# Graph attention, layer 1: the ELU's and the residual's sums on GpSimd, row terms by transfers, maxima over more tiles, and a mask operation over two key tiles

## The reference, cut to what matters

```python
Wh = jnp.einsum('bnf,fo->bno', h, W)
s_i = Wh @ a[:Fout, 0]
s_j = Wh @ a[Fout:, 0]
e = leaky_relu(s_i[:, :, None] + s_j[:, None, :], negative_slope=0.2)
e = jnp.where(mask, e, -jnp.inf)          # mask: adj > 0, or i == j
attention = softmax(e, axis=-1)
h_prime = jnp.einsum('bij,bjo->bio', attention, Wh)
x = _layernorm(x + elu(h_prime))
```

## Time and profile before

| | us |
|---|---|
| median of 3 runs (lowest, highest) | 3980.1 (3978.75, 3983.96) |
| the profiled execution | 3980.02 |
| its span | 3978.2 |
| VectorE busy | 3254.2 (82%) |
| TensorE busy | 3643.7 (92%) |
| ScalarE busy | 2520.5 (63%) |
| GpSimd busy | 2064.1 (52%) |

### The profile page before, as it was taken

One profiled execution on the slowest core, in us unless ns is written; L12 is line 12 of the kernel. 1 busy time (PEld: TensorE's weight loads), 2 busy tenths in 40 slices (PEclk: granted clock), 3 DMA queues, 4 the chain that ended last, 5 costly groups with the idle time before them and its releaser, 6 DMA issues. The chain is left out here.

```text
span 3978.2 us, 135900 instructions
## 1 busy us (share of the span) xinstructions
PE 3643.7 (92%) x57428; PEld 2511.2 (63%) x57428; DVE 3254.2 (82%) x3989; ACT 2520.5 (63%) x3554; POOL 2064.1 (52%) x1068
## 2 busy tenths in 40 slices
PE   6999999999999999999999999942998998999898
PEld 2656756655756655665665675522776777777777
DVE  6786887787788688688788778857989989889897
ACT  3666666666666666666666666622677676776777
POOL 1786787777678687678677768831101011011010
PEclk9999999999999999999999999976999999999999
DMA  6010010010010001001001000042111110110101
GB/s 216 3 37 16 14 40 14 19 35 19 14 40 14 14 19 40 14 14 40 18 15 35 19 14 19 19 164 78 39 43 33 44 54 24 52 54 22 33 28 37
DMA packets 106692, 145.28 MB, mean 37 GB/s; under 512 B 3792, under 2 KB 87632, under 8 KB 104016
## 3 DMA queue, kind: packets, MB, share of 16 engines
q1 hardware_dynamic: 104816, 135.80, 10.2%
q10 hardware_dynamic: 1248, 0.40, 0.1%
HBM read 102.63 MB, written 33.55 MB: 34 GB/s over the span
## 5 line engine op out<-in xcount | busy, mean ns | idle before, releaser
L277 POOL TENSOR_TENSOR psums<-probs 128x1024 f32<-128x1024 f32 x512 | 1288.8, 2517 | 626.7 <-ACT probs L381 624.4
L381 ACT ACTIVATE probs<-probs 128x1024 f32<-128x1024 f32 x1024 | 1083.5, 1058 | 812.8 <-DVE probs L857 791.2
L493 PE MATMUL ctx_ps<-probs,v_rows 64*32 64x512 f32 x16256 | 1477.1, 590 | 11.7 <-DVE seg_ctx L780 10.3
L857 DVE SCALAR_TENSOR_TENSOR probs<-sc_ps,clip_hi 128x1024 f32<-128x1024 f32 x1024 | 1225.0, 1216 | 217.6 <-PE sc_ps L480 206.6
L480 PE MATMUL sc_ps<-q_cols,k_cols 64*32 64x512 f32 x16384 | 1205.0, 592 | 43.9 <-DVE probs L857 43.3
L1324 PE MATMUL out_ps<-wh,e 128*128 128x257 f32 x4096 | 963.7, 388 | 166.0 <-DVE e L1466 157.2
L1324 PEld LDWEIGHTS out_ps<-wh,e 128*128 128x128 f32 x4096 | 777.5, 193 | 326.6 <-DVE e L1466 117.9
L493 PEld LDWEIGHTS ctx_ps<-probs,v_rows 64*32 64x32 f32 x16256 | 664.0, 106 | 289.9 <-issue 190.6
L480 PEld LDWEIGHTS sc_ps<-q_cols,k_cols 64*32 64x32 f32 x16384 | 533.8, 106 | 333.9 <-issue 212.2
L1153 POOL TENSOR_TENSOR rstd<-var_eps,minus_half 128x4 f32<-128x4 f32 x32 | 68.4, 2138 | 1069.6 <-DVE var_eps L1426 1069.6
L487 PE MATMUL den_ps<-psums,ones 64*32 64x512 f32 x4064 | 598.3, 594 | 17.9 <-DVE seg_ctx L780 11.2
(11 more groups left out here) (97 smaller groups left out, 3356.1 us busy)
## 6 DMA issues: line engine op xcount, KB each, us to landing
x_cols<-in_xT SPq DMA_DIRECT2D x8, 2048.0 KB, 7.9
probs<-in_adjT SPq DMA_DIRECT2D x16, 1024.0 KB, 8.4
x_rows<-in_x SPq DMA_DIRECT2D x32, 512.0 KB, 4.1
x<-res SPq DMA_DIRECT2D x32, 512.0 KB, 2.9
x_in<-x SPq DMA_DIRECT2D x8, 2048.0 KB, 10.3
x_res<-x SPq DMA_DIRECT2D x32, 512.0 KB, 4.7
out<-h SPq DMA_DIRECT2D x32, 512.0 KB, 3.2
e<-in_adjT SPq DMA_DIRECT2D x8, 1024.0 KB, 7.8
```

The source lines that it names most:

```text
L277: pool.tensor_tensor(psums[:, q % 2, pair, :], probs[:, (SJ * q) % RING, pair, :], probs[:, (SJ * q + 1) % RING, pair, :], ALU.add).then_i ...
L381: act.activation(probs[:, n % RING, pair, :], probs[:, n % RING, pair, :], ACT.Exp, scale=DH ** -0.5).then_inc(s_exp, 1)
L493: return pe.matmul(ctx_ps[quad(h), z, :], v_rows[head_rows(r), n % JB, at:at + QUAD], probs[head_rows(r), n % RING, h, :], start=start, st ...
L857: dve.scalar_tensor_tensor(out=probs[:, n % RING, pair, :], in0=sc_ps[:, p, :, :], scalar=-LIM, in1=clip_hi[:, j, c * CW:(c + 1) * CW][:, ...
```

## The change

```diff
-    AHEAD = 3
+    AHEAD = 4
+    LARGER_AHEAD = 2
-    TU, WU, SU = KB * NC, JB, NC
-    uses_at = [1 + u for u in range(TU)] + [10 + 27 * j // JB for j in range(JB)] \
-        + [37 + 2 * c for c in range(NC)]
-    TAKEN = 4
+    TU, WU = KB * NC, JB
+    uses_at = [1 + u for u in range(TU)] + [9 + 27 * j // JB for j in range(JB)]
+    TAKEN = 3
-    LATE = 3
+    LATE = 2
+    EARLY = 2
     def max_at(j):
-        return 17 + 27 * j // JB
-    ROWS_AT = (53, 55, 57, 59)
+        return 13 + 33 * j // JB
+    INV_AT, STATS_AT, VAR_AT, OFFSET_AT = 2, 9, 9, 10
+    SCALE_AT, EXP_AT, NORM_AT = 2, 4, 13
+    ROWS_AT = 51
...
+            def spread_own(b):
+                sp.wait_ge(s_prepread, count(b, USES, 2 + TU + WU))
...
+                    sp.dma_start(s_d[0].rearrange("(j p) -> p j", p=P), wh[:, b[1] % 2, :, 0]).then_inc(s_sout, 16)
+                sp.wait_ge(s_sout, count(b, 16, 16))
+                sp.dma_start(s_c[:, :], s_d[0].rearrange("(p j) -> p j", p=P)).then_inc(s_sin, 16)
+            def make_rows(b):
+                p = b[1] % 2
+                sp.wait_ge(s_all, count(b, 1, 1))
+                sp.dma_start(m_c[:, :], low[0:1, p, :].rearrange("o (q j) -> o q j", j=RJ)).then_inc(s_m, 16)
+                sp.wait_ge(s_rows, count(b, 4, 4))
+                sp.dma_start(rows_d.rearrange("r (p j) -> p r j", p=P), rows_c[:, :, :]).then_inc(s_rout, 16)
+                sp.wait_ge(s_rout, count(b, 16, 16))
+                sp.dma_start(best[:, p, :], rows_d[0].partition_broadcast(P)).then_inc(s_rin, 16)
+                sp.dma_start(low[:, p, :], rows_d[1].partition_broadcast(P)).then_inc(s_rin, 16)
...
+                    if c == 2 and more:
+                        spread_own(following(b))
+                    if c == NC - 1 and more:
+                        make_rows(following(b))
...
+            def elu_and_residual(b, c):
+                own = h[:, c % 2, :, :]
+                pool.wait_ge(s_min, count(b, NC, c + 1))
+                pool.sem_inc(s_waited, 1)
+                pool.tensor_tensor(own, own, neg[:, :, :], ALU.add).then_inc(s_pos, 1)
+                pool.wait_ge(s_en, count(b, NC, c + 1))
+                pool.wait_ge(s_xr[c % 2], count(b, 16 * (NC // 2), 16 * (c // 2 + 1)))
+                pool.sem_inc(s_waited, 1)
+                pool.tensor_tensor(x_res[:, c % 2, :, :], x_res[:, c % 2, :, :], e_neg[:, :, :], ALU.add)\
+                    .then_inc(s_elu, 1)
+                pool.wait_ge(s_pos, count(b, NC, c + 1))
+                pool.wait_ge(s_elu, count(b, NC, c + 1))
+                pool.sem_inc(s_waited, 1)
+                pool.tensor_tensor(own, own, x_res[:, c % 2, :, :], ALU.add).then_inc(s_r, 1)
...
             order = [(j, (0, 1)) for j in range(LATE)] + [(j, (2, 3)) for j in range(LATE)] \
-                + [(j, range(T)) for j in range(LATE, JB)]
+                + [(j, range(T)) for j in range(LATE, JB - EARLY)] \
+                + [(j, (2, 3)) for j in range(JB - EARLY, JB)] + [(j, (0, 1)) for j in range(JB - EARLY, JB)]
...
             def row_operation(b, k):
-                    dve.tensor_tensor(low[:, p, :], low[:, p, :], s_row[:, :], ALU.add).then_inc(s_rows, 1)
+                    dve.wait_ge(s_sin, count(b, 16, 16))
+                    dve.wait_ge(s_m, count(b, 16, 16))
+                    dve.tensor_tensor(m_c[:, :], m_c[:, :], s_c[:, :], ALU.add).then_inc(s_rows, 1)
...
-            def elu(b, c):
-            def residual(b, c):
...
-                        if n + 1 < STEPS:
-                            larger_side(b, n + 1)
+                        if n + LARGER_AHEAD < STEPS:
+                            larger_side(b, n + LARGER_AHEAD)
-                        dve.wait_ge(s_max, count(b, STEPS, LRING + n + 1))
-                        dve.scalar_tensor_tensor(out=tile, in0=mask[:, j, c * CW:(c + 1) * CW], scalar=0.0,
-                                                 in1=tile, op0=ALU.max, op1=ALU.min).then_inc(s_e, 1)
+                        if j % 2 == 0:
+                            tiles = e[:, n % ERING:n % ERING + 2, :]
+                            dve.wait_ge(s_max, count(b, STEPS, LRING + n + 2))
+                            dve.scalar_tensor_tensor(out=tiles, in0=mask[:, j:j + 2, c * CW:(c + 1) * CW],
+                                                     scalar=0.0, in1=tiles, op0=ALU.max, op1=ALU.min).then_inc(s_e, 2)
```

More of the change, by code:

```diff
@@ L1207, in sides @@
                 if n == 0:
-                    act.wait_ge(s_rows, count(b, 4, 4))
+                    act.wait_ge(s_rin, count(b, 32, 32))
                     act.wait_ge(s_fifths, count(b, 1, 1))
@@ L1226, in exp_h @@
                 act.wait_ge(s_h, count(b, NC * T, 2 * T + T * (c + 1)))
+                act.wait_ge(s_pos, count(b, NC, c))
                 act.activation(neg[:, :, :], h[:, c % 2, :, :], ACT.Relu, scale=-1.0).then_inc(s_min, 1)
                 act.wait_ge(s_min, count(b, NC, c + 1))
-                act.activation(neg[:, :, :], neg[:, :, :], ACT.Exp, scale=-1.0).then_inc(s_en, 1)
+                act.wait_ge(s_elu, count(b, NC, c))
+                act.activation(e_neg[:, :, :], neg[:, :, :], ACT.Exp, scale=-1.0).then_inc(s_en, 1)
             def norm_h(b, c, t):
@@ L1289, in prepare @@
                     for k in range(KB):
-                        last = pe.matmul(prep_ps[:, u % 2, 0:F + 1], x_cols[:, k, j * P:(j + 1) * P],
+                        last = pe.matmul(prep_ps[:, u % 2, 0:F + 2], x_cols[:, k, j * P:(j + 1) * P],
                                          w_ext[:, k, :], start=(k == 0), stop=(k == KB - 1))
[L1292 to L1297, removed]
                 last.then_inc(s_prep, 1)
@@ L1341, in _ @@
             for k in range(KB):
-                for i, (row, dst) in enumerate(((a1_r, wa1[:, k:k + 1]), (a2_r, w_ext[:, k, 0:1]))):
-                    dve.tensor_tensor_reduce(out=trash[:, 2 * k + i, :], in0=w_ext[:, k, 1:F + 1], in1=row[:, :],
+                for i, (row, dst) in enumerate(((a1_r, w_ext[:, k, 0:1]), (a2_r, w_ext[:, k, 1:2]))):
+                    dve.tensor_tensor_reduce(out=trash[:, 2 * k + i, :], in0=w_ext[:, k, 2:F + 2], in1=row[:, :],
                                              scale=1.0, scalar=0.0, op0=ALU.mult, op1=ALU.add,
                                              accum_out=dst).then_inc(s_wa, 1)
[L1346 to L1350, removed]
             def mask_piece(i):
@@ L1446, in prologue @@
                     row_operation((0, 0), k)
-                larger_side((0, 0), 0)
+                for n in range(LARGER_AHEAD):
+                    larger_side((0, 0), n)
             def larger_side(b, n):
@@ L1486, in steps @@
                                 fifths(following(b))
-                            if n in ROWS_AT:
-                                row_operation(following(b), ROWS_AT.index(n))
+                            if n == ROWS_AT:
+                                for k in range(4):
+                                    row_operation(following(b), k)
             def tail(b):
@@ L1505, in build @@
     layer0(nc, x, xT, adjT, wqT, wkT, wvT, woT, bq, bk, bv, bo, gamma, beta, x1)
-    layer1(nc, x1, adjT, W, a, out)
+    s_d = nc.dram_tensor("s_own", (1, x.shape[1]), F32, kind="Internal").ap()
+    rows_d = nc.dram_tensor("rows", (2, x.shape[1]), F32, kind="Internal").ap()
+    layer1(nc, x1, adjT, W, a, s_d, rows_d, out)
 def kernel(x, adj, L0_gnn_Wq, L0_gnn_bq, L0_gnn_Wk, L0_gnn_bk, L0_gnn_Wv, L0_gnn_bv, L0_gnn_Wo, L0_gnn_bo,
```

109 lines of the change are left out of this document (54 added, 55 removed).

## The result

The changed kernel takes 4016.8 us (median of 4, 4013.1 to 4020.6) against 3980.6 (3978.8 to 3984.0): 1.009 times as long, 95% interval 1.0073 to 1.0108. That is 36 us slower. The forecast was 3986, no change that can be measured, and the time lies 0.8 us above the end of the range. The profiled execution took 4013.1 with a span of 4011.1.

What follows compares the result with a forecast made beforehand. VectorE was taken to bound chunks 2 and 3, TensorE chunk 0 and the start of chunk 1. From 3980.0 us, - 9 (first seven batches) + 5 (last batch) + 7 (prologue) + 3 (tail) gave 3986, range 3940 to 4016.

Steps and rivals of the forecast that it cites:

- prologue, reduction to the first step: Before layer 1's steps: 9.3 us becomes 16.3, +7, bounds +3 (with a 2 MB load of 6) and +12.
- chunk 0, six times: Chunk 0 of each batch after the first: 28.3 us becomes 32.9, +28 over six.
- chunks 1 to 3, seven times: Chunks 1 to 3 of seven batches: 126.9 us becomes 121.3 a batch, -39 over seven.
- last batch: Four chunks at 29.3 us for 27.1, +8.8, less 4 for TensorE ending closer behind VectorE's last mask: +5.
- the hold: Layer 1: each GpSimd sum keeps VectorE's two-SBUF-input operations standing for 2.2 us, twelve a batch: +26.4 us.
- plain sum: VectorE's work in a batch: masks -2.0, ELU and residual -9.1, row operations -8.4, together -19.5 us.
- I count no further idle: Chunks 0 and 1: TensorE's backlog of 35.5 us against 32.9 fits in VectorE's lead of up to 4 steps.
- (a): Statistics at j = 9: VectorE idles 1.3 us in chunks 0 and 3 and all of the last batch.
- (b): Row operations at n = 51: VectorE idles 1.9 us behind reduction and small DMA, bounds 0 and 3.2.
- Late chain by way of HBM: Rival: m_c or rows land late, VectorE stands at n = 51 and step 0; 4018 us, chance 0.18.
- Holds fall where VectorE waits anyway: Rival: holds in chunk 0 and each chunk's first fall in VectorE's idle time; 3948 us, chance 0.29.
- Pairs starve TensorE: Rival: paired masks are ready 1.1 us later, about 0.5 a step pair at worst in chunks 1 to 3; no chance given.

Runs made afterwards that it cites:

- experiment 1: The changed kernel with ELU and residual back on VectorE at j = 6 and j = 8, all else kept: 3912.7 us.
- experiment 2: The changed kernel with GpSimd's three sums cut to 128x4, the rest of ELU and residual left out: 3888.9 us.
- experiment 5: The changed kernel with GpSimd's three sums turned into fills of the same tiles, ELU and residual left out: 3880.1 us.
- experiment 7: The changed kernel with the four row operations at n = 54 instead of 51: 4007.5 us.
- experiment 9: The kernel of experiment 7 with statistics and variance at j = 12, offset at 13 and norm from 14: 4003.3 us.
- experiment 6: The changed kernel without GpSimd's reduction over the partitions (maximum a constant 40), its small operation ahead and the two loadings: 3945.1 us.
- experiment 11: The changed kernel with ELU and residual on VectorE and single masks, leaving the row terms' transfers and new places: 3918.3 us.
- experiment 3: The changed kernel with one mask operation for each key tile again: 4028.8 us.
- experiment 4: The kernel before with paired masks alone, with AHEAD 4 and LARGER_AHEAD 2: 3968.1 us.

## Why the prediction was wrong

Each part in one table. The spans' difference is 32.9 us. The chunks are counted from larger side to larger side, the tail from the last larger side to the end.

| term | forecast | measured |
|---|---|---|
| before the prologue's reduction | 0 | -3.9 |
| prologue, reduction to the first step | +7 | +2.4 |
| first chunk 0 | +2 | +4.5 |
| chunk 0, six times | +28 | +26.8 |
| chunks 1 to 3, seven times | -39 | -10.8 |
| last batch | +5 | +11.2 |
| tail | +3 | +2.7 |
| sum | +6 | +32.9 |

**Right: the hold and its size.** VectorE's plain sum was right (19.5 us a batch less; its busy time without the holds falls by 19.0, mean of six batches), and it was given back through SBUF. A VectorE operation with two SBUF inputs stands still while a GpSimd sum reads: seen in operations of 2.42, 4.46 and 2.83 us, taken away in experiments 1, 2 and 5. Chunk 1 came out at 45.8 to 46.0 in four of seven batches, and the forecast was 45.9. It took 46.7 in the first and 48.6 in two others, which are longer than their neighbours in the kernel before as well (51.1 and 52.9 for 49.9); there ScalarE stands for up to 4.7 us for nothing that the profile shows. In a full queue three sums cost 6.5 us (chunk 2: 43.5 here, 37.0 with fills in experiment 5), 2.2 each. The mean of 1.5 is lower since in chunk 0 (held 3.3 us of 6.6) and in chunk 3 (full holds in four batches, none in three) half of them fall where VectorE waits.

**Wrong, the step that failed: "I count no further idle", and waits (a) and (b).** I put 4.5 us of idle time on a batch (1.3, 1.3, 1.9). Measured, VectorE idles 16.5 us a batch (chunks 0 to 3: 6.6, 1.7, 0.4, 7.8; means over six batches). That is 12.0 us more, and holds of 21.4 instead of 29.8 (both with the reduction's) give 8.4 back: 3.6 us a batch more than forecast, 25 in seven. Chunk 1 has little part in it (it falls by 3.7 us a batch in the mean, 4.0 forecast). In three pieces:

- *Chunk 2, 43.5 for 41.1.* I placed maxima by n and the windows by larger sides, which run two steps ahead. So chunk 2 has seven maxima and not six (in its window L1423 is busy 18.6 us, 16.4 without its hold). The one too many in my chunk 0 had raised VectorE to 31.6 there. Without it VectorE would need 29.3 there with full holds, and it was busy for 26.1; TensorE binds instead, and 2.3 us moved out of a chunk that couldn't give them back. Chunk 0 came out at 32.7 for a forecast of 32.9, but by another engine than I had: TensorE is busy for 32.80 of 32.80.
- *Chunk 3, 35.4 to 36.2 for 34.3.* The wait for m_c is 4.1 and not 1.9, although the DMA lands in 2.0 us instead of 2.7. From the last maximum's end to m_c it takes 17.0 us where I had 15.0: GpSimd's small operation ahead of the reduction stands behind a larger side and a mask (1.74 in the batch shown, for which I had 0.3 with all handing over), and the reduction takes 7.5 in the mean and not 6.1. And I counted GpSimd's pause ahead of the reduction but not the one behind it, 7.5 us more for the first sum. Experiments 7, 9 and 6 show the two waits one behind the other: move the first alone and 1.3 to 1.6 of 4.1 us come in; take the reduction away and chunk 3 loses 7.1.
- *Last batch, +11.2 for +5.* A chunk takes 29.6, near my 29.3, and the first 31.0. But the 4 us that I took off for TensorE's lag at the end did not come: it ends 6.4 us behind VectorE's last mask, as before (6.7, for which I had 7.5).

**The rivals.** "Late chain by way of HBM" gave 4018 and the time is 4017, but it is right by its number only. VectorE does stand at n = 51, for 4.1 us, but not for the reason it named: m_c lands in 2.0 us, the rows are stored in 1.5 and loaded in 6.9, no engine waits for them at step 0 in the seven batches' steps, and the transfers with the new places are a gain (experiment 11). What is late is GpSimd itself, its reduction and the pauses around it. "Holds fall where VectorE waits anyway" is true for about a third of them, and it didn't help, since waits and holds then take turns. "Pairs starve TensorE" is out (experiments 3 and 4).

**Prologue.** 17.8 us from the reduction's start to ScalarE's first step, 15.4 before. I had bounded small transfers from below by 2.7; they land in 1.5 to 2.0, and the rows come back in 6.9 where I had 9.5. So it rises by 2.4 us and not by 7, below my bound of 3:

```profile
best<-rows SPq DMA_DIRECT2D x8, 1024.0 KB, 4.4
low<-rows SPq DMA_DIRECT2D x8, 1024.0 KB, 6.9
m_c<-low SPq DMA_DIRECT2D x8, 8.0 KB, 2.0
rows<-rows_c SPq DMA_DIRECT2D x8, 16.0 KB, 1.5
s_own<-wh SPq DMA_DIRECT2D x7, 8.0 KB, 10.8
s_c<-s_own SPq DMA_DIRECT2D x7, 8.0 KB, 1.7
```

The 3.9 us that the first row of the table has lie in layer 0 and its handover, which hardly change; the prologue's reduction starts at 2736.6 here, at 2740.6 before and at up to 2746.8 in the experiments, none of which touches layer 0. So I take it for the spread between executions.

**Open.** How the 7.1 us of chunk 3 divide between the reduction's own hold, the reload and the wait for m_c was not separated further: leaving out the reduction takes all three, and experiment 7 shows only that the last is worth 2.3 of chunk 3 by itself. Nor was it separated whether chunk 0 has more of TensorE's work left over because the clock is lower in chunk 3 (0.87, and 1.00 in experiment 6, where chunk 0 is 1.5 us shorter).

## What to carry to other kernels

Before moving an elementwise sum to GpSimd to unload VectorE, look at what VectorE runs beside it: if most of that has two SBUF inputs, the move costs VectorE nearly the GpSimd operation's whole length where its queue is full (2.2 us for the 1.14 us taken off), and where one input comes from PSUM, as in the earlier trace rows, nothing that the trace shows. Here GpSimd's queue paid 6 us at the switch from a sum to a reduction over the partitions and 7.5 at the switch back (a fill paid nothing there), so latency-bound work should not stand behind one. When two waits stand one behind the other, test them together: alone the move of the rows gave 9 us, with the second wait gone 35.

## What was not expected of the hardware

- A GpSimd fill of 128x1024 takes 0.95 us, does not hold VectorE, and starts directly behind a reduction; a sum of the same size takes 2.36 and starts 7.5 us behind it. The Trainium skill, page "GPSIMD Engine Reference", section "2.1 Instruction dispatch", states about 6 us for a first call after a load; if the pauses are such loads, the trace agrees ahead of the reduction (5.98), and behind it it is 1.5 more.
- 2048 values of 4 bytes from 128 partitions to HBM land 10.8 us after their issue, as long as 2 MB in pieces of 1 KB (10.4). A row of 8 KB spread over 128 partitions, twice, is there after 6.9.
- A GpSimd operation on four values (the power, L1190) takes up to 3.22 us where VectorE has just started a maximum, 1.02 in the tail: a tiny operation too waits for its turn. The larger side and the mask behind that maximum take 0.69 and 1.21, so it held neither.
